# A four-unit loop on TensorE, and GpSimd without waits for landing beside the expert units

## The reference

```python
x = conv_attention(x)                  # full attention over each image's 1024 pixels
x = iterative_whitening(x)
t = to_tokens(x)
t = t + linear_attention(layernorm(t))
t = t + moe_gelu(layernorm(t))         # 8 experts, top 2, 128 -> 512 -> 128
t = t + window_attention(layernorm(t)) # windows of 32 tokens, 4 heads
t = t + moe_silu(layernorm(t))         # 8 experts, top 2, gated, 128 -> 341 -> 128
```

## Time and profile before

| | us |
|---|---|
| median of three runs | 1704.69 (1699.76 to 1714.86) |
| the profiled execution's own time | 1710.91 |
| its span, first to last instruction | 1709.0 |
| gelu units, first to last transpose of a unit | 531.9 to 866.6 |
| silu units, first to last transpose of a unit | 1310.6 to 1633.1 |

### The profile page before, as it was taken

One profiled execution on the slowest core, in us unless ns is written; L12 is line 12 of the kernel. 1 busy time (PEld: TensorE's weight loads), 2 busy tenths in 40 slices (PEclk: granted clock), 3 DMA queues, 4 the chain that ended last, 5 costly groups with the idle time before them and its releaser, 6 DMA issues. The chain is left out here.

```text
span 1709.0 us, 31908 instructions
## 1 busy us (share of the span) xinstructions
PE 1306.3 (76%) x11786; PEld 1095.5 (64%) x11786; DVE 986.9 (58%) x2376; ACT 522.9 (31%) x1183; POOL 594.1 (35%) x640
## 2 busy tenths in 40 slices
PE   6999987075764888898975786846754999999960
PEld 3555566075753888898963454624444999999960
DVE  3777755998562334365536444662245677687851
ACT  3444420021622444444432221421131232322230
POOL 4000000241155665545015330055302662355654
PEclk9999998588557999999986665666655999999985
DMA  7500000001212333333232210011001332333341
GB/s 279 229 0 1 1 4 1 3 1 36 82 36 74 101 104 104 97 100 101 80 82 62 63 27 2 1 36 41 26 2 39 106 110 82 90 104 100 105 140 52
DMA packets 87889, 115.45 MB, mean 68 GB/s; under 512 B 18694, under 2 KB 70274, under 8 KB 87746
## 3 DMA queue, kind: packets, MB, share of 16 engines
q1 hardware_dynamic: 66786, 62.73, 11.9%
q0 software_dynamic: 20960, 50.76, 9.5%
HBM read 53.01 MB, written 60.42 MB: 66 GB/s over the span
## 5 line engine op out<-in xcount | busy, mean ns | idle before, releaser
L1304 POOL DMA_INDIRECT sorted_rows<-s_normed,s_places x128 | 137.7, 1076 | 220.8 <-POOLq L2404 89.9
L1380 POOL DMA_INDIRECT sx_fetch<-sorted_results,s_places x128 | 132.6, 1036 | 145.8 <-DMA sx_fetch<-sorted_results,s_places 59.9
L1380 POOL DMA_INDIRECT gx_fetch<-sorted_results,g_places x128 | 127.5, 996 | 128.0 <-DMA gx_fetch<-sorted_results,g_places 61.5
L1304 POOL DMA_INDIRECT sorted_rows<-g_normed,g_places x128 | 130.2, 1017 | 114.7 <-DMA sorted_rows<-g_normed,g_places 50.3
L1463 PE MATMUL g_bank<-weights,gx_hT 128*128 x1360 | 168.6, 278 | 0.0
L1463 PEld LDWEIGHTS g_bank<-weights,gx_hT 128*128 128x128 f32 x1360 | 161.8, 195 | 0.2 <-issue 0.2
L1428 PE MATMUL s_bank<-sx_xT_high,sx_w_now 128*128 128x256 f32 (+1 forms) x510 | 151.2, 297 | 2.4 <-DVE sx_hT L1533 1.8
L1430 PE MATMUL s_bank<-sx_xT_high,sx_w_now 128*128 128x256 f32 (+1 forms) x510 | 143.7, 282 | 0.0
L1429 PE MATMUL s_bank<-sx_xT_low,sx_w_now 128*128 128x256 f32 (+1 forms) x510 | 143.6, 281 | 0.0
L1463 PE MATMUL s_bank<-weights,sx_hT 128*128 (+1 forms) x1020 | 131.7, 279 | 8.9 <-issue 4.9
L1488 ACT ACTIVATE gx_hT<-g_bank,gx_b_now 128x256 f32<-128x256 f32 x340 | 133.6, 486 | 3.6 <-PE g_bank L1463 3.6
(11 more groups left out here) (404 smaller groups left out, 2895.8 us busy)
## 6 DMA issues: line engine op xcount, KB each, us to landing
sorted_rows<-zeros POOLq DMA_DIRECT2D x29, 512.0 KB, 16.6
gx_xq<-sorted_rows SPq DMA_DIRECT2D x85, 128.0 KB
sorted_results<-gx_yq SPq DMA_DIRECT2D x85, 128.0 KB
sx_xq<-sorted_rows SPq DMA_DIRECT2D x85, 128.0 KB
sorted_results<-sx_yq SPq DMA_DIRECT2D x85, 128.0 KB
feats<-in_x SPq DMA_DIRECT2D x8, 512.0 KB, 5.1
out<-s_normed SPq DMA_DIRECT2D x16, 256.0 KB
g_raw_up<-in_L_ffn_W SPq DMA_DIRECT2D x1, 2048.0 KB, 9.0
```

The lines of the kernel that those rows point to most:

```text
L1304: pool.indirect_dma_start(out=sorted_rows[g], out_offset=bass.IndirectOffsetOnAxis(ap=places[:, at, r:r + 1], axis=0), in_=normed[:, at, : ...
L1380: pool.indirect_dma_start(out=fetch[n % 2][:, i, r, :], out_offset=None, in_=self.sorted_results[g], in_offset=bass.IndirectOffsetOnAxis(a ...
```

## The change

TensorE's 89 steps become 8 written steps, a loop `Fori(2, 21)` of 19 turns with four steps in each, and 5 written steps. The functions `go_up`, `turn` and `go_down` get the buffer numbers apart from the unit's number, which in the loop is worked out from the register. The products and the order of work are the same. GpSimd's `send_group` and `bring` get a switch, `pauses`, which is off for all that GpSimd does beside units, in both blocks; it stays on in the two routings and for gelu's group 2.

```diff
--- before.py
+++ after.py
@@ -1297,14 +1297,14 @@
         steps.settle()
 
 
-def send_group(pool, plan, g, normed, places, sorted_rows, sent):
+def send_group(pool, plan, g, normed, places, sorted_rows, sent, pauses=True):
 
     for at in range(plan.first_tile[g], plan.first_tile[g + 1]):
         for r in range(2):
             pool.indirect_dma_start(
                 out=sorted_rows[g], out_offset=bass.IndirectOffsetOnAxis(ap=places[:, at, r:r + 1], axis=0),
                 in_=normed[:, at, :], in_offset=None).then_inc(sent[g], 16)
-        if at % 2 == 1:
+        if pauses and at % 2 == 1:
             pool.wait_ge(sent[g], (at + 1 - plan.first_tile[g]) * 2 * 16)
 
 
@@ -1364,7 +1364,7 @@
         self.added_both = t.sem(f"{tag}added_both")
         self.tiles_added = 0
 
-    def bring(self, pool, groups):
+    def bring(self, pool, groups, pauses=True):
         places, fetch, fetched = self.places, self.fetch, self.fetched
 
         plan = self.plan
@@ -1381,7 +1381,7 @@
                             out=fetch[n % 2][:, i, r, :], out_offset=None, in_=self.sorted_results[g],
                             in_offset=bass.IndirectOffsetOnAxis(ap=places[:, n * SEND + i, r:r + 1], axis=0)
                             ).then_inc(fetched[n % 2], 16)
-                    if i % 2 == 1:
+                    if pauses and i % 2 == 1:
                         pool.wait_ge(fetched[n % 2], (n // 2 * SEND + i + 1) * 2 * 16)
 
         for g in groups:
@@ -1429,11 +1429,10 @@
             pe.matmul(out, left[:, part, columns], right[1][:, :], start=False, stop=False)
             pe.matmul(out, left[:, part + 1, columns], right[0][:, :], start=False, stop=True)
 
-        def go_up(u):
-            i = u % 2
+        def go_up(u, i):
             pe.wait_ge(xT_ready, u + 1)
             pe.wait_ge(self.w_ready, u + 1)
-            if u >= 2:
+            if not (isinstance(u, int) and u < 2):
                 pe.wait_ge(hT_ready, u - 1)
             for k, (at, width) in enumerate(chunks):
                 for m in range(kind.products):
@@ -1445,34 +1444,45 @@
                         out = up[i][2][0:width, m, :]
                     product(out, w_now[i], xT[i], 2 * m, slice(at, at + width))
 
-        def turn(u):
-            pe.wait_ge(self.x_loaded[u % 4], (u // 4 + 1) * 16)
-            if u >= 2 - alone:
+        def turn(u, i, q, loads):
+            pe.wait_ge(self.x_loaded[q], loads * 16)
+            if not (isinstance(u, int) and u < 2 - alone):
                 pe.wait_ge(xT_ready, u - 1 + alone)
             for k in range(KT):
-                done = pe.transpose(turned[u % 2][:, P * k:P * k + P], self.xq[u % 4][:, k, :], self.ident[:, :])
+                done = pe.transpose(turned[i][:, P * k:P * k + P], self.xq[q][:, k, :], self.ident[:, :])
             return done
 
-        def go_down(u):
-            e = pe.value_load(self.owners[0:1, u:u + 1], min_val=0, max_val=E - 1)
+        def go_down(u, i):
+            e = pe.value_load(self.owners[0:1, bass.ds(u, 1)], min_val=0, max_val=E - 1)
             pe.wait_ge(hT_ready, u + 1)
-            if u >= 2 - alone:
+            if not (isinstance(u, int) and u < 2 - alone):
                 pe.wait_ge(y_ready, u - 1 + alone)
             for k in range(KT):
-                for i, (_, width) in enumerate(chunks):
-                    done = pe.matmul(down[u % 2][:, P * k:P * k + C], hT[u % 2][0:width, i, P * k:P * k + P],
-                                     self.w_down[0:width, bass.ds(e, 1), i, :].rearrange("p a c -> p (a c)"),
-                                     start=(i == 0), stop=(i == len(chunks) - 1))
+                for n, (_, width) in enumerate(chunks):
+                    done = pe.matmul(down[i][:, P * k:P * k + C], hT[i][0:width, n, P * k:P * k + P],
+                                     self.w_down[0:width, bass.ds(e, 1), n, :].rearrange("p a c -> p (a c)"),
+                                     start=(n == 0), stop=(n == len(chunks) - 1))
             return done
 
-        for s in range(self.STEPS):
+        def step(s):
             if 0 <= s - self.TO_UP < self.NU:
-                go_up(s - self.TO_UP)
+                go_up(s - self.TO_UP, s % 2)
             if s < self.NU:
-                done = turn(s)
+                done = turn(s, s % 2, s % 4, s // 4 + 1)
             if s >= self.TO_DOWN:
-                done = go_down(s - self.TO_DOWN)
+                done = go_down(s - self.TO_DOWN, s % 2)
             done.then_inc(self.stepped, 1)
+
+        fours = self.NU // 4
+        for s in range(8):
+            step(s)
+        with pe.Fori(2, fours) as four:
+            for j in range(4):
+                go_up(four * 4 + j - self.TO_UP, j % 2)
+                turn(four * 4 + j, j % 2, j, four + 1)
+                go_down(four * 4 + j - self.TO_DOWN, j % 2).then_inc(self.stepped, 1)
+        for s in range(4 * fours, self.STEPS):
+            step(s)
 
     def scalar(self, act):
         kind, chunks, up, xT, hT, silu = self.kind, self.kind.chunks, self.up, self.xT, self.hT, self.silu
@@ -2223,8 +2233,8 @@
         @block.gpsimd
         def _(pool):
             for g in range(1, plan.groups):
-                send_group(pool, plan, g, normed, places, group_rows, sent)
-            units.bring(pool, range(plan.groups - 1))
+                send_group(pool, plan, g, normed, places, group_rows, sent, pauses=False)
+            units.bring(pool, range(plan.groups - 1), pauses=False)
             units.wait_for_stores(pool)
             silu_setup.clear(pool)
             units.bring(pool, [plan.groups - 1])
@@ -2465,8 +2475,8 @@
         @block.gpsimd
         def _(pool):
             for g in range(1, plan.groups):
-                send_group(pool, plan, g, normed, places, group_rows, sent)
-            units.bring(pool, range(plan.groups))
+                send_group(pool, plan, g, normed, places, group_rows, sent, pauses=False)
+            units.bring(pool, range(plan.groups), pauses=False)
 
         @block.tensor
         def _(pe):
```

## The result

The change makes the kernel slower: 1966.38 us, median of four runs (1944.6 to 1974.2), against 1707.11 for the kernel before in the same comparison; ratio 1.148, interval 1.136 to 1.159. The ratio leaves out the slowest of the four, 1974.2, which lies over 1.5% above the fastest. The profiled execution took 1944.6 us, its span 1942.7: 233.7 more than before.

The account below looks back on a forecast made before the run. Late signals beside units (excess 37 us) and GpSimd's fetches behind silu's last unit were taken as what the change could improve. 1710.91 - 17 - 15 + 6 = 1684.9, against the median 1678 us; range 1650 to 1715.

Parts of the forecast that it names:

- The pauses' term: Beside gelu and silu units: dropping GpSimd's pauses lets late signals come sooner, -15 us, bounds -37 and 0.
- I take -15: The gain in us chosen for dropping GpSimd's pauses beside the units, between bounds of -37 and 0.
- something other than the DMAs themselves is needed: Beside the units: the reason for -15 us, that runs of DMAs alone don't make TensorE's steps slower.
- The signal rival: Beside units: longer runs of GpSimd's DMAs hold TensorE's signal `stepped` longer, +59 us in sum, 1764 us; chance 0.12.
- Runs of DMAs also stand beside silu's 3.70 without harm: Silu's 28 steps beside sends keep 3.70 us a step, the argument against runs of DMAs holding signals.
- The tail: Fetch behind silu's last unit: shorter intervals, 10.0 us less, and an earlier start, 7 less; -17 us, bounds -10 and -18.3.
- the first part: Silu's last group: without pauses the 23 intervals of its 24 DMAs take 29.0 us instead of 39.0, 10.0 less.
- The loop: TensorE's unit loops: back edges and register instructions cost +6 us, lower bound 0, perhaps 20 at most.
- TensorE's code: TensorE's instruction fetch: 56 code packets instead of 96, worth 0 us.
- Code fetched again at each back edge: TensorE's unit loops: each of 38 turns fetches two packets anew, 2.3 us a turn, +87 us, 1765 us; chance 0.08.

Follow-up runs that it names:

- Experiment 8: Looped kernel with all pauses plus 64 extra back-to-back GpSimd DMAs after silu's sends, against the kernel before: plain 1728.81 us (1.012), indirect 1791.32 us (1.060).
- experiment 9: Kernel before, written out, pauses dropped only for silu's last group, against the kernel before: ratios 1.000 (0.997 to 1.003) and 0.998 (0.995 to 1.001).

## Why the prediction was wrong

The time lies far outside the range of 1650 to 1715.

- **The pauses' term: wrong in sign and size.** The step that failed is "I take -15", with its bounds of -37 and 0. It left the loss to a rival, at 0.12. The runs showed the opposite in its place: written-out code without pauses measures +13.7%, about +232 us, with the tail's gain in it. In that trace the units alone, which is where the term stands, take 467.5 us in gelu (528.0 to 995.5) and 439.6 in silu (1434.5 to 1874.1), +132.8 and +117.1: +250 where -15 was written. Its reason was that "something other than the DMAs themselves is needed". Experiment 8 shows that nothing else is: indirect DMAs back to back suffice. A pause is a wait of GpSimd alone, but it is what lets TensorE's signals through.
- **The signal rival: right in mechanism, too small in price.** It said that runs of DMAs hold `stepped`, and named its signs, unnamed waits beside GpSimd's DMAs and a pace above 4.5. But it was priced with the worst pace in the rows, 4.49, as if every run were like the runs of four there. The measured pace is 5.4 beside runs of eight, and none to speak of beside runs of 64 and 96. It missed that TensorE's own issue crawls too. The trace of before did say it: all nine late signals come through behind the fourth DMA of a run, none earlier in it, and an average over short runs can't bound a long one.
- **"Runs of DMAs also stand beside silu's 3.70 without harm"** was the argument against. It was true for runs of four with a gap behind each (in silu's sends of before, 1340 to 1420 us, 1.78 us a DMA on average), and says nothing of runs without one.
- **The tail: mechanism right, size near.** In the changed kernel the last group's DMAs start at 1901.70 and 1932.49, 30.8 us in place of 39.0 (29.0 were forecast), and they start 21.9 us behind the last transpose in place of 27.5. That is 8.2 + 5.6 = 13.8 where 10.0 + 7 was forecast; the stretch from the last transpose to the end is 13.0 shorter. Timed by itself, the first part isn't clear of the noise (experiment 9).
- **The loop: right.** +6 forecast within 0 to 20; +8.4 in one trace, +14 timed (6 to 22), so its size was somewhat low.
- **TensorE's code: right.** 56 packets as forecast, and no run shows a worth of them: the loop as a whole costs a little.
- **Code fetched again at each back edge: didn't happen**, 0 of 38 branches over 0.22 us. The rule on taken branches of the Trainium skill ("Runtime: NRT & Kernel Launch", section "Instruction fetch mechanics") doesn't bite for a turn of 302 instructions on TensorE; its figure of 2048 instructions for TensorE's own store agrees with that.

## What to carry to other kernels

A wait that seems to guard nothing may be what spaces a stream, so find out what it keeps apart before it goes. When a disturbance appears only late in short bursts, don't price longer bursts with the pace beside short ones: it can go on growing with the length of the run. In this kernel, with indirect DMAs of 128 rows of 512 bytes, one every 1.5 us and runs of four with a gap behind them cost little, and plain DMAs needed no such care. Where indirect DMAs run beside TensorE, look for unnamed waits of the engines that it signals, and try a gap before a higher rate. None of the ways of spacing tried here beat the pauses that were there.

## What the runs showed of the hardware

- Indirect DMAs of GpSimd at one every 1.26 us starve TensorE: its semaphore signals come up to 58.5 us late, and its matmuls start 0.7 to 2.8 us apart, in steps of 0.7 us, at a granted clock of 0.50 to 0.51, its 1.2 GHz level. VectorE's and ScalarE's own instructions keep their durations (0.42 and 0.39 us at lines 1554 and 1491). Only TensorE's signals are seen late: in the same run of DMAs VectorE's copy ends at 1458.22 and SyncE issues the store that waits for it at 1458.25. With a memset after each DMA, signals at 1.47 us a DMA are a little late (31 times in gelu, none in silu), at 1.73 never.
- The state takes some DMAs to build up: in the silu sends of the changed kernel, which begin with the units, the first signal that is 5.9 us late follows the step that ended at 1451.9, 17 us into the run. It outlasts the run by about 12 us in gelu. In runs of four a signal is held as well: ScalarE waits up to 4.6 us for it, and it comes through 1.9 to 2.1 us after the fourth DMA's start.
- Plain DMAs of GpSimd every 0.60 us, at 178 GB/s with all other traffic, have no such effect, in the same queue and with as many packets for each.
- By what way indirect DMAs reach TensorE isn't shown. The late signals and the late matmuls may be one thing, a last matmul that is recorded but not done; no run tells these apart.
- A loop of four steps on TensorE costs 0.2 us of sequencer time for its branch; timed, the two loops of 19 turns cost 14 us (6 to 22). Code packets fall from 96 to 56, and none came from 1367 to 1472 us, beside silu's loop, where 8 came before.
